# Scores of a 64-token block attention: from zero-padded keys in full-array products to four groups of 32 rows side by side

## The reference

```
h = layernorm(x) * (1 + ca) + sa
q, k, v = split(h @ W_qkv.T + b_qkv, 3); q = q * 16**-0.5
qb, kb, vb = blocks of q, k, v                # (8, 16 heads, 8 blocks, 64 tokens, 16)
attn = softmax(einsum('bhnld,bhnmd->bhnlm', qb, kb))
out = einsum('bhnlm,bhnmd->bhnld', attn, vb) @ W_out.T + b_out
x = x + ga * out
...                                           # coupling net, three cycles
...                                           # second layer: attention over 512 tokens, 8 heads of 64,
...                                           # with lookahead scores; then 8 experts, top-k tokens each
```

## The kernel before

```
+kq:1 proj:1.4 turn_vu:0 +sc0:0 +wt0:0 +sc0:1 +wt0:1 +v:0 -attend:10 +v:1 +sc0:2 +wt0:2 +tp0:0 +sc0:3 proj:1.3
+tp0:1 -turn:11 +wt0:3 -x1_load:0 proj:1.1 +sc0:4 +tp0:2 +sc0:5 +tp0:3 +wt0:4 +wt0:5 +pv0:0 w:0.0 ...
```

## Time and profile before

| | us |
|---|---|
| median of 3 runs | 1942.61 (1941.24 to 1942.82) |
| the profiled execution | 1942.89 |
| its span, first to last instruction | 1941.6 |
| TensorE busy | 1910.8, 11192 records |
| VectorE / ScalarE / GpSimd busy | 1110.0 / 929.4 / 718.7 |
| mean granted TensorE clock | 0.995 of full |

### The profile page before, as it was taken

One profiled execution on the slowest core, in us unless ns is written; L12 is line 12 of the kernel. 1 busy time (PEld: TensorE's weight loads), 2 busy tenths in 40 slices (PEclk: granted clock), 3 DMA queues, 4 the chain that ended last, 5 costly groups with the idle time before them and its releaser, 6 DMA issues.

```text
span 1941.6 us, 30468 instructions
## 1 busy us (share of the span) xinstructions
PE 1910.8 (98%) x11192; PEld 1316.7 (68%) x11192; DVE 1110.0 (57%) x2904; ACT 929.4 (48%) x2034; POOL 718.7 (37%) x833
## 2 busy tenths in 40 slices
PE   8989999999999999999999999999999999999998
PEld 5735656666665566566666655656876788888887
DVE  6768676668556655756675665586344547223221
ACT  5646666556646564655565566354244421111111
POOL 3303335334433433353343324343344424333332
PEclk9989999999999999999999999999999999999999
DMA  4020001000000100010010000040130224333333
GB/s 129 1 101 1 12 11 29 23 1 20 20 23 1 39 1 23 1 39 22 1 39 1 23 2 14 33 166 1 30 85 12 66 58 100 64 76 79 85 77 70
DMA packets 59697, 76.78 MB, mean 40 GB/s; under 512 B 7120, under 2 KB 52824, under 8 KB 59296
## 3 DMA queue, kind: packets, MB, share of 16 engines
q1 hardware_dynamic: 46448, 57.28, 9.0%
q0 software_dynamic: 12288, 16.79, 5.1%
q10 hardware_dynamic: 816, 0.79, 0.1%
HBM read 53.71 MB, written 21.00 MB: 38 GB/s over the span
## 4 chain that ended last, share of the span: by engine, by line
PE 96%; DVE 2%; ACT 1%; issue 1%; DMA 0%; POOL 0%; ACTq 0%; DVEq 0%; POOLq 0%
PE bank L766 14%; PE bank L979 11%; PE bank L992 11%; PE bank L829 7%; PE bank L780 4%; PE bank L884 4%; PE bank L865 4%; PE bank L853 4%; PE bank L618 3%; PE bank L592 3%; PE bank L838 3%; PE bank L751 3%; PE bank L897 3%; PE bank L816 2%; PE bank L713 2%; PE bank L644 2%
## 5 line engine op out<-in xcount | busy, mean ns | idle before, releaser
L1229 ACT ACTIVATE h<-bank 128x512 f32<-128x512 f32 x128 | 76.5, 598 | 346.6 <-PE bank L979 337.1
L979 PE MATMUL bank<-xin,ew 128*128 128x256 f32 x1024 | 234.6, 381 | 0.0
L992 PE MATMUL bank<-ew,h 128*128 128x256 f32 x1024 | 226.9, 379 | 0.0
L992 PEld LDWEIGHTS bank<-ew,h 128*128 128x128 f32 x1024 | 194.2, 190 | 26.4 <-issue 0.2
L979 PEld LDWEIGHTS bank<-xin,ew 128*128 128x128 f32 x1024 | 189.6, 190 | 24.9 <-issue 1.8
L1806 POOL DMA_INDIRECT out<-y,indices x64 | 103.0, 1610 | 278.5 <-DVE y L1665 181.4
L1768 POOL TENSOR_TENSOR s<-s,ri 128x256 f32<-128x256 f32 (+3 forms) x128 | 160.1, 1264 | 111.9 <-DVE ri L1528 111.9
L1205 ACT ACTIVATE s<-s,mn 128x128 f32<-128x128 f32 (+3 forms) x256 | 141.5, 554 | 121.2 <-DVE mn L1521 121.1
L1506 DVE SCALAR_TENSOR_TENSOR th<-th,bank 128x384 f32<-128x384 f32 (+1 forms) x192 | 104.9, 595 | 126.7 <-ACT th L1196 126.5
L1665 DVE SCALAR_TENSOR_TENSOR y<-bank,gates,gbe 128x256 f32<-128x256 f32 x64 | 30.9, 484 | 244.2 <-PE bank L992 240.3
L829 PE MATMUL bank<-look,term 128*128 128x384 f32 (+3 forms) x512 | 153.1, 436 | 0.1
(11 more groups left out here) (318 smaller groups left out, 3668.6 us busy)
## 6 DMA issues: line engine op xcount, KB each, us to landing
ew<-L_ffn_w SPq DMA_DIRECT2D x24, 1024.0 KB
x1s<-x_scratch SPq DMA_DIRECT2D x8, 512.0 KB, 5.2
out<-x1s SPq DMA_DIRECT2D x8, 512.0 KB, 2.9
xn_scratch<-n_xn SPq DMA_DIRECT2D x8, 512.0 KB
x<-L_attn_x SPq DMA_DIRECT2D x7, 512.0 KB, 3.9
x_scratch<-x SPq DMA_DIRECT2D x7, 512.0 KB, 2.9
wqkv<-w_qkv SPq DMA_DIRECT2D x1, 3072.0 KB, 9.9
wqkv<-L_wmod SPq DMA_DIRECT2D x2, 1024.0 KB, 8.8
```

The source lines that it names most:

```text
L979: mm = te.matmul(banks[i][:, g * 2 * P:(g + 1) * 2 * P], w1[:, kk, (2 * n + g) * P:(2 * n + g + 1) * P], xin[:, kk, :, :].rearrange("p h s ...
L992: mm = te.matmul(banks[i][:, 0:D], ex.h1[:, g, n * P:(n + 1) * P], w2[:, g, :], start=(g == 0), stop=(g == FC - 1))
```

## The change

Four blocks at a time, and no padding.

- `f.k` becomes [128, KC, NBLK, LB]; the two fills of the padding (L1694 and the four ScalarE instructions for `k0b`) go, and the keys are written by one instruction of 128 rows instead of four of 32.
- `sc0` is now a step per four blocks, two per batch. For block m, chunk c and group r it multiplies the 32 partitions of group r: 128 query columns as weights, 64 key columns streaming. That is 32 products per step. Group r writes into a bank of its own, so one step fills four banks, and each holds the scores of four blocks for two heads of each chunk.
- What VectorE and ScalarE did under `sc0` is a step of its own, `sm0`, eight per batch, one per bank; its work per bank is the same size as before. `wt0` and `tp0` follow `sm0`.
- `pv0` has the same eight products over four blocks and two groups, and its eviction goes to other columns.
- The three tables are written anew, for this and for all other steps; the counts of the other steps are the same.

The diff without the tables:

```diff
@@ -242,7 +242,7 @@
 
 
 
-PRODUCTS = {"feat": KC, "kq": 2, "v": 1, "sc0": 1, "tp0": 1, "pv0": 1, "setup0": 1, "out0": 1, "gc": 1, "twist": KC,
+PRODUCTS = {"feat": KC, "kq": 2, "v": 1, "sc0": NR, "tp0": 1, "pv0": 1, "setup0": 1, "out0": 1, "gc": 1, "twist": KC,
             "cn2": 1, "cn3": 1, "cn4": 2, "fin0": NT // 2, "vc": 1, "proj": 1, "look": 2, "term": 2, "su": 2, "sc": 2, "turn": 2, "turn_vu": 1, "w": 1,
             "out1": 1, "feat_t": KC, "gate": 1, "probs": 1, "pos": 1, "index": 1, "turn_x": 1, "hidden": 1,
             "output": 1, "cols": 1}
@@ -362,7 +362,7 @@
     def __init__(self, nc, name, x, ga, norm, hT, early, sb):
         self.x, self.ga, self.norm, self.hT = x, ga, norm, hT
         self.tmp = norm.xn[:, 0:2, :]
-        self.k = early(f"k0{name}", [P, KC, NBLK, NR, LB])
+        self.k = early(f"k0{name}", [P, KC, NBLK, LB])
         self.v = early(f"v0{name}", [P, NBLK, NR, 64])
         self.q = sb(f"q0{name}", [P, KC, NBLK, 2, LB])
         self.s = [sb(f"s0{name}{i}", [P, NR, KC, LB]) for i in range(2)]
@@ -612,12 +612,19 @@
                     for which in range(2):
                         i, nth = at["kq", b, c, which]
                         te.wait_ge(drained[i], nth)
-            i, nth = at[step, b, n, 0]
-            te.wait_ge(drained[i], nth - 1)
-            for c in range(KC):
-                mm = te.matmul(banks[i][:, c * 256:(c + 1) * 256], f.q[:, c, n, :, :].rearrange("p a l -> p (a l)"),
-                               f.k[:, c, n, :, :].rearrange("p r m -> p (r m)"), start=True, stop=True)
-            mm.then_inc(full[i], 1)
+            for r in range(NR):
+                i, nth = at[step, b, n, r]
+                te.wait_ge(drained[i], nth - 1)
+            for m in range(2 * KC):
+                for c in range(KC):
+                    col = (KC * m + c) * LB
+                    for r in range(NR):
+                        rows = slice(32 * r, 32 * r + 32)
+                        i, nth = at[step, b, n, r]
+                        mm = te.matmul(banks[i][:, col:col + LB], f.q[rows, c, 4 * n + m, :, :].rearrange("p a l -> p (a l)"),
+                                       f.k[rows, c, 4 * n + m, :], start=True, stop=True)
+                        if (m, c) == (2 * KC - 1, KC - 1):
+                            mm.then_inc(full[i], 1)
 
         elif step == "tp0":
             i, nth = at[step, b, n, 0]
@@ -638,11 +645,10 @@
                 te.wait_ge(drained[i], nth)
             i, nth = at[step, b, n, 0]
             te.wait_ge(drained[i], nth - 1)
-            for blk in range(2):
-                for r in range(NR):
-                    col = 2 * blk + r // 2
-                    mm = te.matmul(banks[i][HALVES[r % 2], col * P:(col + 1) * P], f.v[:, 2 * n + blk, r, :],
-                                   f.pT[blk][:, r, :], start=True, stop=True)
+            for blk in range(4):
+                for j in range(2):
+                    mm = te.matmul(banks[i][HALVES[j], blk * P:(blk + 1) * P], f.v[:, 4 * (n // 2) + blk, 2 * (n % 2) + j, :],
+                                   f.pT[j][:, blk, :], start=True, stop=True)
             mm.then_inc(full[i], 1)
 
         elif step == "out0":
@@ -1019,12 +1025,11 @@
                 a.dma_start(b0.bk[:, :], bq[1]).then_inc(done, 16)
 
             a.wait_ge(s["const_pool"], N_POOL_CONST)
-            for whole in (k.first[1].v[:, :, :, :].rearrange("p n r e -> p (n r e)"),
-                          k.first[1].k[:, :, :, :, :].rearrange("p c n r m -> p (c n r m)")):
-                for col in range(0, whole.shape[1], 8 * P):
-                    a.activation(whole[:, col:col + 8 * P].rearrange("p (i j) -> p i j", j=P),
-                                 k.const.ident[:, :].unsqueeze(1).to_broadcast([P, 8, P]), ACT.Identity, scale=0.0
-                                 ).then_inc(s["zeroed"], 1)
+            whole = k.first[1].v[:, :, :, :].rearrange("p n r e -> p (n r e)")
+            for col in range(0, 16 * P, 8 * P):
+                a.activation(whole[:, col:col + 8 * P].rearrange("p (i j) -> p i j", j=P),
+                             k.const.ident[:, :].unsqueeze(1).to_broadcast([P, 8, P]), ACT.Identity, scale=0.0
+                             ).then_inc(s["zeroed"], 1)
 
         elif step == "setup":
             a.wait_ge(s["wqkv_in"], 48)
@@ -1061,27 +1066,22 @@
         elif step == "kq":
             i, nth = at[step, b, n, 0]
             a.wait_ge(full[i], nth)
-            if b == 1:
-                a.wait_ge(s["zeroed"], 6)
-            for r in range(NR):
-                rows = slice(32 * r, 32 * r + 32)
-                done = a.activation(f.k[rows, n, :, r, :], banks[i][rows, :].rearrange("p (n m) -> p n m", m=LB),
-                                    ACT.Identity, bias=b0.bk[rows, n:n + 1])
-            done.then_inc(drained[i], 1)
+            a.activation(f.k[:, n, :, :], banks[i][:, :].rearrange("p (n m) -> p n m", m=LB), ACT.Identity,
+                         bias=b0.bk[:, n:n + 1]).then_inc(drained[i], 1)
 
         elif step == "v":
             i, nth = at[step, b, n, 0]
             a.wait_ge(full[i], nth)
             if b == 1:
-                a.wait_ge(s["zeroed"], 6)
+                a.wait_ge(s["zeroed"], 2)
             for c in range(KC):
                 rows = slice(64 * c, 64 * c + 64)
                 out = f.v[rows, 4 * n:4 * n + 4, :, :].rearrange("p n r (a c e) -> p (n r) a c e", a=2, c=KC)
                 done = a.copy(out[:, :, :, c, :], banks[i][rows, :].rearrange("p (g a e) -> p g a e", a=2, e=HD0))
             done.then_inc(drained[i], 1)
 
-        elif step == "sc0":
-            i, nth = at[step, b, n, 0]
+        elif step == "sm0":
+            i, nth = at["sc0", b, n // NR, n % NR]
             a.wait_ge(drained[i], nth)
             a.activation(f.s[n % 2][:, :, :, :], f.s[n % 2][:, :, :, :], ACT.Exp).then_inc(f.sem["exp0"], 1)
 
@@ -1098,9 +1098,8 @@
             a.wait_ge(full[i], nth)
             for quarter in range(4):
                 rows = slice(32 * quarter, 32 * quarter + 32)
-                done = a.copy(f.aT[rows, :, n * P:(n + 1) * P].rearrange("p k (b l) -> p b k l", b=2),
-                              banks[i][rows, :].rearrange("p (b k a l) -> p b k a l", b=2, k=KC, a=2)[
-                                  :, :, :, quarter % 2, :])
+                done = a.copy(f.aT[rows, n % 2, n // 2 * 4 * LB:(n // 2 + 1) * 4 * LB].rearrange("p (b l) -> p b l", b=4),
+                              banks[i][rows, :].rearrange("p (b a l) -> p b a l", b=4, a=2)[:, :, quarter % 2, :])
             done.then_inc(drained[i], 1)
 
         elif step == "gc":
@@ -1388,10 +1387,9 @@
             if n >= 2:
                 j, old = at["tp0", b, n - 2, 0]
                 v.wait_ge(full[j], old)
-            v.tensor_tensor(sc[:, :, :, :].rearrange("p r c m -> p c r m"),
-                            banks[i][:, :].rearrange("p (c r m) -> p c r m", c=KC, r=NR),
-                            mx[:, :].rearrange("p (c r) -> p c r", c=KC).unsqueeze(3).to_broadcast([P, KC, NR, LB]),
-                            ALU.subtract).then_inc(drained[i], 1)
+            v.tensor_tensor(sc[:, :, :, :].rearrange("p b c m -> p (b c) m"),
+                            banks[i][:, :].rearrange("p (g m) -> p g m", m=LB),
+                            mx[:, :].unsqueeze(2).to_broadcast([P, NR * KC, LB]), ALU.subtract).then_inc(drained[i], 1)
 
         elif step == "wt0":
             g = lap * NBLK + n
@@ -1690,8 +1688,7 @@
     g.memset(c_.sign[:, :], 1.0).then_inc(done, 1)
     select(c_.sign[:, :], ALU.is_ge, -1.0, P // 2 - 1, 0, 1, -1, 9)
     g.memset(c_.power[:, :], -0.5).then_inc(done, 2)
-    g.memset(k.first[0].v[:, :, :, :], 0.0)
-    g.memset(k.first[0].k[:, :, :, :, :], 0.0).then_inc(s["setup_pool"], 1)
+    g.memset(k.first[0].v[:, :, :, :], 0.0).then_inc(s["setup_pool"], 1)
     g.wait_ge(done, N_POOL_CONST)
 
     def inverse_root(norm, mv, rstd, nth):
```

More of the change, by code:

```diff
@@ L83 @@
-    +bias0:0 term:0 look:0.1 look:0.2 look:0.3 +kq:0 +kq:1 proj:1.4 turn_vu:0 +sc0:0 +wt0:0 +sc0:1 +wt0:1 +v:0
-    -attend:10 +v:1 +sc0:2 +wt0:2 +tp0:0 +sc0:3 proj:1.3 +tp0:1 -turn:11 +wt0:3 -x1_load:0 proj:1.1 +sc0:4 +tp0:2
-    +sc0:5 +tp0:3 +wt0:4 +wt0:5 +pv0:0 w:0.0 -attend:11 w:0.1 +pv0:1 +tp0:4 +sc0:6 +tp0:5 su:0 su:1 -o_out:3 +wt0:6
-    +pv0:2 sw:0 sw:1 proj:1.0 vc:0 sc:0 weigh:0 sc:1 look:1.0 +sc0:7 +tp0:6 +wt0:7 -out1:0 -out1:1 -stats_t:0
-    -norm_t:0 +tp0:7 vc:1 turn:0 weigh:1 proj:1.2 vc:2 turn_vu:1 vc:3 su:2 sw:2 look:1.1 look:1.2 look:1.3 sc:2
@@ L88 @@
-    term:1 attend:0 w:1.0 +pv0:3 w:1.1 turn:1 -feat_t:0 +out0:0 +out0:1 proj:2.0 su:3 +stats:1 attend:1 sw:3 weigh:2
-    +norm:1 sc:3 -gate:0 proj:2.1 +feat:1 turn:2 su:4 attend:2 sw:4 sc:4 +cn1:0 +twist:0 +gc:0 +cn2:0 o_out:0
```

(13 more changed lines are left out.)

148 lines of the change are left out of this document (74 added, 74 removed).

## The result

The changed kernel takes **1945.87 us** (median of 11; 1942.97 to 1948.55) against 1941.29 for the kernel before, a ratio of 1.0021 (1.0012 to 1.003). Forecast was 1925, range 1917 to 1938: wrong in size, and in sign by a little.

The account below looks back on a forecast made before the run. TensorE, busy 98% of the span, was taken to bound the kernel except at the start. Scores -27.2, switches +5.0, head +2.5 and new waits +2.0 gave -17.7 us, from 1942.9 to about 1925 us; range 1917 to 1938.

Parts of the forecast that it names:

- The scores themselves: Scores products on TensorE: 1.78 us per four-block step, 28.4 us for 16 steps instead of 55.6, saving 27.2 us.
- How many groups work at once: Within the scores products: four row groups run at once, 16 rounds of 0.111 us per step.
- Switches: Changes of the TensorE array's shape: 482 instead of 449, at 0.15 us each, +5.0 us (3 to 8).
- Keys: Key writes: one ScalarE instruction instead of four, 33 us less ScalarE work, no gain in the period.
- Zeroing: Fills of the padded keys at the start go: m0sil ends 3.5 us earlier, gain 0, at most 1 us.
- Head: Start, 34 to 98 us: four scores steps save 6.8 us of TensorE, part returns as waiting, +2.5 us (0 to 6).
- The stretch from 98 to 142 ... stays, clock drops included: Late part of the start, 98 to 142 us: a chain of other engines, unchanged.
- Waits that are new: Softmax starts only after a four-block step, so transposes come 0.1 to 0.3 us late; +2.0 us over 16 steps (0 to 8).
- Rival 3, "banks": Scores steps: 1.1 us more each waiting for four free banks or late softmax units, 1943 us (1938 to 1950); chance 8%.

Follow-up runs that it names:

- experiment 4: Changed kernel with the scores step's loop order and row groups varied over batches 4 to 7: 1983.69 us (one execution), only step times of use.
- experiment 1: Changed kernel's order, four-block steps and banks, but with the old padded keys and full-array products: 1968.07 us, ratio 1.0141 against the kernel before.
- experiment 3: Changed kernel, but with order, padded keys and full-array products of the kernel before for batches 0 to 2: 1933.54 us, ratio 0.9959.
- the mixed one: Old order, padded keys and products for batches 0 to 2, changed kernel after, feat_t behind both out0 steps: 1932.77 us; with 83 useless transposes in its head 1929.96.

## Why the prediction was wrong, step by step

- **"The scores themselves"**: right. A step takes 1.94 us with a switch. "How many groups work at once": four, shown by experiment 4. Against the 3.65 us of a step in experiment 1 that is 1.71 us each, 27.4 over the 16 steps, forecast 27.2. Only 22.2 of it came out in the time. That this equals 27.2 - 5.0 is chance, since experiment 1 has most of the new switches too. What is missing is 3.2 us before batch 1's `proj` (six steps saved 7.1 there, not 10.3) and 0.6 in each period, of which 0.37 is the wait ahead of the first transpose.
- **"Switches"**: the counts are nearly right. The shapes in the traces change 445 times before, 481 after (449 and 482 counted), and 474 in experiment 1. The 0.15 us of one was not tested by itself.
- **"Keys", "Zeroing"**: right. m0sil takes 1.33 us (3.33 to 4.66), the first product starts at 5.64, the second group of products still at 13.17; ScalarE is down by 35 us.
- **"Head", put at +2.5 us (0 to 6)**: this step failed. In the prediction's own terms, the stretch up to batch 1's `proj` has six steps (6 x -1.69), 13 switches (+2.0), six of the sixteen waits (+0.8) and this +2.5: -4.9. It measured +11.4, so the term came to about 19 and not 2.5. I counted what four of the sixteen steps save and how much VectorE has to do, and asked only whether the saved time comes back as waiting. I didn't ask when the units come to VectorE. The order costs 18.6 us up to batch 1's `proj` (experiment 1), of which the products give back 7.1: +11.4 net. With useless transposes in both heads, batch 1's `proj` starts at 320.4 in the changed order and at 312.4 in the old one. So 3.4 us of the 11.4 went with the clock, and 8.0 are left (profiled executions, one of each kernel; the first `proj` of the same head has come at 152.2 and at 155.0). These hold some clock still: 13.6 us at half clock against 3.4, which can cost 5 us at most. The remainder is when the units come, the bursts. That experiments 1 and 3 put the loss into the new order of the head is shown. That within it the bursts are the cause is read from the timeline and the windows; the new tables also move other steps, and no run made bursts in the old order by themselves.
- **"The stretch from 98 to 142 ... stays, clock drops included"**: failed. It starts 6.7 us later, and its windows have a lower clock.
- **"Waits that are new", +2.0 over 16 steps**: the mechanism was right in the period (0.37 us ahead of the first transpose, 0.1 to 0.3 forecast), but a greater wait was elsewhere in the same order, and I had put nothing for it: `feat_t`, 1.5 us per period (moving it got 0.6 back). The period came to 176.5, forecast 174.5 to 175.0; 174.5 + 1.5 + 0.37 is 176.4. The 2.2 us per period of experiment 1 are the same 1.5 and four more switches (59 against 55, 0.6 by the forecast's price); the 0.37 us are not in it: its first units start early, and its first transposes do not wait.
- **Luck**: the last stretch gained 5.8 us, where two steps, waits and no switch gave 3.1. Without the 2.7 us that the new order happened to gain there the miss would have been larger.
- **Rival 3, "banks"**, with 1938 to 1950 us and 8%, gave the right time and half the mechanism, and was priced as an even 1.1 us per step, while the loss sat in the head. The units do come late since four banks fill at once. But TensorE waited little for free banks (1.7 us in the head; eight banks: no gain that can be told). By the program's rotation banks act earlier, in that they limit the order: a second step of four can't be put forward by a place, because it needs banks that are only drained after a transpose that would then stand behind it, while with single blocks the old order could feed VectorE one by one. This is argued from the program; no run shows it.

## What to carry to other kernels

A step that produces four units at once saves on the engine that makes them and starves or floods the one that takes them; list the start times of the consumer's units, not only its busy sum. Where a stage is not bound by TensorE, leave its fine grain alone and use the coarse step only where it is: here the old head with the new steps behind it gave 1933.5. And before blaming a chain of waits, hold the clock once with useless products in the idle places: it shows how much of the loss is clock, as far as the clock then stays up.

## What the hardware showed that I had not expected

- Full-array transposes that nothing uses, put into idle places, made three kernels 2.5 to 5.5 us faster; the half-clock time of the changed head went from 37.5 to 10.2 us, that of the mixed one from 13.6 to 3.4.
- The granted clock fell from its full 2.4 GHz to half while TensorE worked without a gap in one quarter of its array (the windows at 894.95 and 899.40), as it does behind waits; with four quarters at work in the periods it stayed. The kernel before has such a fall too, 3.4 us at 1112.2, with only 0.16 us idle in the 12 us ahead of it, where products on half of the array and products of 8 columns stand.
- Two products of one group next to each other cost 8% of a step (2.09 against 1.94 us); eight products (sixteen records) in a row undo nearly all of the overlap (7.4 to 7.7 us, part of it at half clock).
